# Latent attention: the reciprocal of the row sums written back into PSUM and read from there, and GpSimd's three head sums added by three instructions

## The reference, cut to what matters

```
q = (x @ wq).reshape(Bq, Tq, N_KV, N_REP, HEAD_DIM)      # 8 heads: 2 groups of 4, 128 features each
k = jnp.einsum('bkhl,ld->bkhd', x @ wk_down, wk_up)      # 2 key heads, rank 32
v = jnp.einsum('bkhl,ld->bkhd', x @ wv_down, wv_up)
scores = jnp.einsum('bqhrd,bkhd->bhrqk', q, k) * scale   # causal mask
probs = jax.nn.softmax(scores, axis=-1)
y = jnp.einsum('bhrqk,bkhd->bqhrd', probs, v)
return y @ wo
```

## Time and profile before

| | |
|---|---|
| median of three executions | 1840.62 us (1838.76 to 1849.7) |
| profiled execution, its own time | 1839.44 us |
| span of its trace | 1837.3 us |
| busy in the span | TensorE 1579.0 us (86%), VectorE 1162.2 (63%), ScalarE 787.1 (43%), GpSimd 802.8 (44%) |
| latent stage | 1385 to 1752 us, 367 us (20% of the span) |
| granted TensorE clock, mean | 0.911 of full speed |

### The profile page before, as it was taken

How to read it: one execution, slowest core, us unless ns; L and a number is a source line. 1 busy time by engine, 2 the same in 40 slices (tenths; PEclk the granted TensorE clock), 3 DMA queues, 4 the chain that set the end, 5 groups by cost and what they waited for, 6 DMA issues and landing times.

```text
span 1837.3 us, 25913 instructions
## 1 busy us (share of the span) xinstructions
PE 1579.0 (86%) x8863; PEld 801.0 (44%) x8863; DVE 1162.2 (63%) x2315; ACT 787.1 (43%) x1031; POOL 802.8 (44%) x987
## 2 busy tenths in 40 slices
PE   4666599869999999999699959998968978898779
PEld 2222366533334333343266636776634333333256
DVE  5888632489878788786243243334268988887841
ACT  2232233263565565556533324444443333444443
POOL 1223663645464636463636363500002546667900
PEclk9788599986999999999889979998988988999979
DMA  5000000141102002000000000000043000000000
GB/s 146 1 0 0 1 1 0 46 117 32 28 2 54 2 5 51 2 3 2 1 1 1 0 0 1 0 0 1 0 137 96 23 23 1 1 1 1 1 6 17
DMA packets 39123, 36.88 MB, mean 20 GB/s; under 512 B 10191, under 2 KB 36272, under 8 KB 38899
## 3 DMA queue, kind: packets, MB, share of 16 engines
q1 hardware_dynamic: 36826, 28.48, 5.5%
q10 hardware_dynamic: 2136, 7.10, 1.8%
q0 software_dynamic: 64, 0.00, 0.0%
HBM read 26.10 MB, written 8.91 MB: 19 GB/s over the span
## 4 chain that ended last, share of the span: by engine, by line
PE 68%; DVE 14%; issue 3%; ACT 3%; POOL 2%; DMA 1%; SPq 0%; DVEq 0%; POOLq 0%; ACTq 0%
PE PS L1374 11%; PE PS L948 10%; PE PS L1322 10%; PE PS L1393 10%; PE PS L936 9%; PE PS L1822 3%; PE PS L1840 3%; DVE sb_rope_mp L1558 3%; POOL sb_H L1480 2%; DVE sb_latent_mp L1558 2%; DVE sb_latent_rec L1588 1%; DVE sb_H L227 1%; PE PS L1834 1%; PE PS L941 1%; PE PS L1351 1%
## 5 line engine op out<-in xcount | busy, mean ns | idle before, releaser
L1558 DVE TENSOR_REDUCE sb_rope_mp<-PS 128x1 f32<-128x512 f32 (+3 forms) x560 | 344.3, 667 | 65.1 <-PE PS L1326 31.3
L1435 ACT ACTIVATE sb_rope_PT<-PS 128x1024 f32<-128x1024 f32 (+3 forms) x320 | 273.4, 895 | 203.8 <-PE PS L1378 104.3
L1000 DVE SCALAR_TENSOR_TENSOR sb_X<-PS,sb_gates,sb_X 128x128 f32 (+1 forms) x320 | 90.1, 344 | 241.2 <-PE PS L948 241.2
L1322 PE MATMUL PS<-sb_rope_K,sb_rope_Q 96*128 96x512 bf16 (+3 forms) x640 | 212.5, 372 | 11.7 <-ACT sb_rope_V L1420 9.6
L581 POOL TENSOR_SCALAR sb_pbelow<-sb_pa,sb_ptrial 128x512 f32<-128x512 f32 x124 | 196.8, 1597 | 6.4
L1558 DVE TENSOR_REDUCE sb_latent_mp<-PS 128x1 f32<-128x512 f32 (+2 forms) x280 | 175.5, 668 | 36.6 <-PE PS L1322 26.7
L588 POOL TENSOR_TENSOR sb_pbelow<-sb_pbelow 128x1024 f32<-128x1024 f32 (+1 forms) x248 | 182.0, 734 | 19.6
L936 PE MATMUL PS<-sb_HT,sb_w 128*128 (+1 forms) x384 | 182.0, 611 | 3.9 <-DVE sb_seed L519 2.3
L1374 PE MATMUL PS<-sb_rope_Q,sb_rope_K 99*128 99x512 bf16 (+3 forms) x640 | 179.4, 352 | 1.4 <-ACT sb_rope_PT L1435 0.9
L1374 PE MATMUL PS<-sb_latent_Q,sb_latent_K 96*128 96x512 bf16 (+7 forms) x640 | 158.8, 369 | 5.4 <-ACT sb_w0b L1435 2.4
L977 ACT ACTIVATE sb_moe_hidden<-PS,sb_vec 128x512 f32<-128x512 f32 x128 | 87.7, 687 | 159.8 <-PE PS L936 155.6
(11 more groups left out here) (315 smaller groups left out, 2716.9 us busy)
## 6 DMA issues: line engine op xcount, KB each, us to landing
sb_latent_Q<-latent_parts SPq DMA_DIRECT2D x48, 128.0 KB, 2.8
sb_rope_Q<-rope_parts ACTq DMA_DIRECT2D x9, 384.0 KB
rope_parts<-sb_rope_parts SPq DMA_DIRECT2D x24, 128.0 KB, 2.4
latent_parts<-sb_latent_parts SPq DMA_DIRECT2D x12, 256.0 KB, 2.6
sb_rope_tab<-in_rotation SPq DMA_DIRECT2D x1, 2048.0 KB, 8.2
sb_rope_K<-rope_parts ACTq DMA_DIRECT2D x6, 256.0 KB
latent_parts<-sb_latent_parts SPq DMA_DIRECT2D x12, 128.0 KB, 2.5
sb_latent_K<-latent_parts SPq DMA_DIRECT2D x48, 32.0 KB, 2.2
```

The source lines that it names most:

```text
L1000: ins = v.scalar_tensor_tensor(xi, k.PS[:, 4 + b:5 + b, i * P:(i + 1) * P], gate, xi, ALU.mult, ALU.add)
L1322: ins = pe.matmul(k.PS[:, bank, at:at + w], self.Q[0:self.rows, g % 2, j, 0, q0:q0 + P], self.K[0:self.rows, g % 2, j % self.kheads, 0, kc ...
L1435: s.activation(self.PT[u % self.B][:, 2 * p:2 * p + 2, q0:CH], k.PS[:, 2 * p:2 * p + 2, q0:CH], ACT.Exp, scale=self.scale).then_inc(self.e ...
L1558: v.tensor_reduce(self.mp[:, n % 2, kc, heads[0]:heads[-1] + 1, i], k.PS[:, bank, 0:len(heads) * w].rearrange("p (h k) -> p h k", h=len(he ...
```

## The change

It has two parts, both in the latent stage. First, the reciprocal of the sums is no longer written to an SBUF tile (rec) but over the sums in the ring bank, and the product reads it from PSUM. The bank is freed after the product, where it was freed after the reciprocal, and VectorE waits for the end of the product before it goes on. Second, an addition of three heads by one instruction on GpSimd becomes three instructions of one head each. The counter added[0] rises by three per unit, and those who wait for it wait for three times the number. VectorE's own head was and is one instruction.

```diff
             if self.summed:
-                pe.wait_ge(self.added[0], self.first_unit(n + 1))
+                pe.wait_ge(self.added[0], 3 * self.first_unit(n + 1))
...
                     if self.summed:
-                        s.wait_ge(self.added[0], u - self.B + 1)
+                        s.wait_ge(self.added[0], 3 * (u - self.B + 1))
...
-            self.add_weights(g, u, 0, slice(0, 3))
+            self.add_weights(g, u, 0, (0, 1, 2))
...
         if u:
-            eng.wait_ge(self.added[who], u)
+            eng.wait_ge(self.added[who], u * len(heads))
         for p in range(who, 2):
             eng.wait_ge(self.exps[p], u + 1)
-        new, acc = self.PT[u % self.B][:, heads, q0:CH], self.acc[n % 2][:, heads, q0:CH]
-        if kj == 0:
-            eng.tensor_copy(acc, new).then_inc(self.added[who], 1)
-        else:
-            eng.tensor_tensor(acc, acc, new, ALU.add).then_inc(self.added[who], 1)
+        for j in heads:
+            new, acc = self.PT[u % self.B][:, j, q0:CH], self.acc[n % 2][:, j, q0:CH]
+            if kj == 0:
+                eng.tensor_copy(acc, new).then_inc(self.added[who], 1)
+            else:
+                eng.tensor_tensor(acc, acc, new, ALU.add).then_inc(self.added[who], 1)
...
-                v.reciprocal(self.rec[:, :], k.bank(bank)).then_inc(free, 1)
-                v.wait_ge(free, uses + 1)
-                v.tensor_tensor(self.On[:, n % 2, :], self.O[:, n % 2, :], self.rec[:, :], ALU.mult) \
-                    .then_inc(self.normed, 1)
+                ch(v.reciprocal(k.bank(bank), k.bank(bank)))
+                ch(v.tensor_tensor(self.On[:, n % 2, :], self.O[:, n % 2, :], k.bank(bank), ALU.mult))
+                v.sem_inc(self.normed, 1)
+                v.sem_inc(free, 1)
```

More of the change, by code:

```diff
@@ L1529, in vector @@
                 if item == "weighted" and self.summed:
-                    self.add_weights(v, u, 1, slice(3, 4))
+                    self.add_weights(v, u, 1, (3,))
                 elif item[0] == "reciprocals":
```

## The result

| | before | after |
|---|---|---|
| median of 19 executions each | 1848.49 us (1837.35 to 1853.99) | 1834.86 us (1827.11 to 1849.59) |
| ratio, after to before | | 0.9949, 95% interval 0.9928 to 0.997 |
| span of the profiled execution | 1837.3 us | 1838.3 us |
| latent stage, GpSimd's first copy to its last addition | 349.87 us | 338.65 us |

The change makes the kernel faster by 0.5%, some 9.4 us (5.5 to 13.3 by the interval). That is about half of the 17.4 that were forecast, and within the 1% that counted as no change; the forecast ratio of 0.990 lies outside the interval. The two medians alone are 13.6 us apart, but the executions of one kernel spread over 17 to 22 us, so I go by the ratio and its interval.

The account below looks back on a forecast made before the run. TensorE bounds most of it, nearly balanced with VectorE in the latent stage, GpSimd in chunk 8; -12.9 - 0.2 - 5.5 - 2.5 + 1.0 + 2.7 = -17.4 us gives 1822.5 us, range 1812 to 1836 (own range 1815 to 1829).

Parts of the forecast that it names:

- product and ring: Latent stage: PSUM product at 0.69 us saves -12.9 us on five products, -0.2 on the first; later bank freeing costs nothing.
- clock: Behind reciprocals 2 to 6: shorter TensorE gaps keep the granted clock up, -5.5 us, bounds 0 and 9.
- casts: Small cast L1571, six times: waits for a GpSimd instruction a third as long, -2.5 us, bounds 0 and -5.4.
- VectorE's additions: Long chunks: they wait for the ends of GpSimd's thirds while GpSimd has no gap, +1.0 us, bounds 0 and +5.
- last chunk: Chunk 8, bound by GpSimd: earlier start gains 1.8 us, units cost more; +2.7 after some overlap, bounds 0 and +6.
- All of it is on the path: Latent stage: the product's saving counts in full, as TensorE waits for VectorE's maxima, -12.9 us and -0.2.
- a third of the instruction, a third of the wait: Cast L1571: waiting for a third of a GpSimd instruction takes a third to a half as long, -2.5 us.
- GpSimd's cost: Three 512-column additions, 1.27 or 1.09 us each, cost GpSimd 0.37 us more per unit, about 28 us busy time.
- The PSUM operand freed the product: Rival said otherwise: product still waits for a third of a GpSimd addition, five cost 3 us more, 1825.5 us; 3%.
- More than forecast: Rival: TensorE's full slow-clock loss of 9 us returns, casts give 4, last chunk costs nothing, 1815.5 us; 14%.
- The slower rival: Chunks 7 and 8: VectorE breaks into each of three GpSimd additions, a unit takes 5.0 us, +10, 1851 us; 10%.
- The first rival: Latent stage: slow clock stays or VectorE bounds at once, clock and cast terms shrink to about -1, 1830 us; 23%.

Follow-up runs that it names:

- the product alone: Only the reciprocal and product moved to PSUM, GpSimd adding three heads in one instruction, against the kernel before: ratio 0.9924, latent stage 333.03 us.
- the chain in PSUM: Full change plus the four small operations on the combined maxima kept in their ring bank, against the kernel before: ratio 0.9906, latent stage 329.49 us.
- In sixths: Full change with each of GpSimd's additions cut once more, six instructions a unit, against the kernel before: ratio 0.9939, latent stage 341.65 us.

## Why the prediction was right in direction and wrong in size

The forecast was 17.4 us, the stretch gives 11.2, and the ratio's 9.4 lies with it inside its interval. On the scale of the forecast, 9.4 us are 1831.2 us: inside the outer range (1812 to 1836), outside the forecast's own (1815 to 1829). The stretch and TensorE's books put the 6.2 us between forecast and stretch as follows. The change is read as a whole here, since its parts meet in the same waits.

| | forecast | measured |
|---|---|---|
| product and ring: TensorE's waits before L1322 and L1351 | -12.9 - 0.2 = -13.1 | -8.2 |
| clock: TensorE's busy time | -5.5 | -8.4 |
| casts: TensorE's wait before L1333 | -2.5 | +1.7 |
| VectorE's additions | +1.0 | inside the first line |
| last chunk | +2.7 | +3.6 |
| sum | -17.4 | -11.3, rounded (stretch: -11.2) |

**The product itself** was right. It is at 687 ns eight times (forecast 0.69), the wait behind it is 1.5 us over six places (forecast 1.2 for five), and the reciprocal is 3.367 us with its output in PSUM, 10 ns more than before. VectorE is rid of 16.1 us in the seven places of the earlier trace rows.

**"All of it is on the path" is the first step that failed.** The prediction booked the product's 13.1 us on the path in full. TensorE's waits for the ring fell by 8.2 us, and by 8.9 with the product alone. Two things in it can be read from the trace. The gap was to be "about 1.2": at the second reciprocal the first gap is 1.09, but two follow it in turn with VectorE, 2.0 us in all. The 1.09 us and the second gap of 0.33 or 0.34 stand in four other kernels as well, so they are no chance. And the later freeing of the bank, costed at nothing, is the first of these gaps, 6.9 us over six places in the stretch. How much of the 6.9 TensorE would have waited anyway isn't shown. VectorE also didn't come free by what it saved on the product: it is busy 63.3 us of the 69.0 afterwards, where it was 61.7, with five products already 14.2 us shorter. Part of what moved in is the wait of its own additions of head 3. They read two operands in SBUF like the old product, and 57 of them take 3.8 us more with the product alone. The prediction had looked at the product and one cast as those that wait for GpSimd, and took the additions for 0.68 us each "mostly". That the 3.8 us are lost on the path one for one was not tested.

**The clock** came back as told, in four windows of five, and by more than the 5.5 us: TensorE's busy time fell by 8.4 us, near the bound of 9. With the product alone it fell by 6.2. The two terms can't be held apart by these runs, since a TensorE that is faster waits longer for VectorE. What is measured for both together is 15.1 us with the product alone, where 18.6 were forecast. That shortfall of 3.5 us is no larger than what two profiles of one program differ by, so its size is not sure, and it could be chance.

**The casts are the second step that failed**, and they went the other way: -2.5 forecast, and TensorE's wait behind the chain rose by 1.7 us. The rule "a third of the instruction, a third of the wait" holds for one instruction. Here four follow each other, each waiting for the one before. With GpSimd unsplit one long instruction held up the first, and the rest slipped through behind it at 174 ns. With thirds, the next third begins while the chain runs, and holds up another of the four, as the lines at 1669.04 show: excess 7.8 us for 5.4. The product alone has the old chain and the old wait of 11.9 us, so it is the split that lengthened them. Putting the chain in PSUM took the excess away and 6.4 us off TensorE's wait, which settles that this wait is on the path.

**GpSimd's cost** was right in the single instruction (1267 and 1086 ns for 1.27 and 1.09) and in its busy time (+28.0 us for "about 28"). In chunk 8, though, three of them in a row take 4.18 us, not 3.81: VectorE's addition still breaks in once a unit, as it did before. Where it doesn't, at 1441.27 us, three take 3.72. A full unit costs 0.40 to 0.44 us more, and the early ones, where several instructions of VectorE fall in, up to 0.95. The split by itself costs 5.3 us in chunk 8, against 4.8 in the forecast before the overlap that I allowed and that didn't come. The start of the chunk gave 1.7 us, read from the product alone; forecast 1.8.

**The rivals.** The clock did not stay down, though with the product alone it came back only in part. The PSUM operand freed the product. "More than forecast" had TensorE's busy time nearly right (9 us, measured 8.4), and the casts and the last chunk wrong. The slower rival, GpSimd as the bound, wanted 4.5 us a unit, and in thirds a unit stays below 4.2. In sixths it takes 4.59 (4.07 with sb_HT); that kernel lost 13.4 us against the product alone in chunk 8, but 0.3 in chunk 7 (66.1 against 65.8), so chunk 7, which has maxima, bears more than the rival said. The first rival's time came nearest: its 1830 is 10.6 us below the median of before, and the gain measured is 9.4 by the ratio. But that is luck, as it let the clock's term shrink to almost nothing and left the product's whole.

By the stretch, the change would have been worth more without its second half. Whether the three instructions help depends on what else is on VectorE: 7.8 us lost in chunks 7 and 8, 0.8 us gained in chunks 1 to 6 of this kernel, which can be chance, and 5.7 to 9.3 us gained there when the chain is out of the way.

## What to carry to other kernels

Where one engine waits for the end of another's running instruction, list every instruction that has this kind of operands, not only the one that stands out: when the worst is mended, the others can be late next, and each of a chain of small ones can wait for a piece of its own once the long instruction is cut. Cut a long instruction only where its engine has idle time: each cut costs its fixed time in full where it hasn't, and that place can be left whole. In a ring between two nearly balanced engines, keep books on the one whose busy time and waits add up to the length, and count a saving on the other by what it takes off these waits. And before small differences of one stage are read from single profiles, look how far two profiles of the same program lie apart.

## What the runs showed of the hardware

An addition of VectorE with two operands in SBUF that started 0.16 us before GpSimd's ran at its full speed (0.68 us), and GpSimd's took 3.28 us where it takes 2.90 undisturbed; started 1.14 us behind, it took 2.31 us and ended 0.55 us after GpSimd's. One with an operand in PSUM is untouched at 128 x 512 (686 to 689 ns) and at 128 x 16 (174 and 182 ns). The small cast has one input only, and still waited when its source and its target were both in SBUF, up to 2267 ns; with its source in PSUM it stayed at 174. The Trainium skill ("SBUF — State Buffer", section "Who interferes with whom") says the same of issue order, and counts copies and casts among those that can contend in their two-port modes; the runs here agree with both. In chunk 8 a cut in a GpSimd addition costs 0.20 us at 512 columns and 0.14 at 256 (4.18 - 3.78 for two cuts, 4.59 - 4.18 for three more). And 2048 columns of four heads take VectorE 2.29 us in one instruction, where GpSimd takes 3.78 us for 1536 (3.44 where VectorE doesn't get in between).
